# Four PSUM banks for maxima and two for scores, with side work moved to other steps, in a fused FFN-attention-FFN kernel

## The reference

```
x = x + 0.5 * ffn(ln(x))
x = x + attention(ln(x))         # 16 heads of 8, softmax(q k^T / sqrt 8) v, biases, output projection
x = x + 0.5 * ffn(ln(x))
ffn(x): h = silu(x W1 s1) * (x W2 s2)       # 128 -> 512, weights -1, 0, 1 with a scale per column
        h = gelu(h H1 sg1); h = gelu(h H2 sg2)        # 512 -> 512
        return h W3 s3                                # 512 -> 128
```

## Time and profile before

| what | us |
|---|---|
| median of 3 runs (lowest, highest) | 622.78 (621.61, 626.68) |
| the profiled execution | 622.23 |
| its span | 620.3 |
| PE busy, PEld busy | 589.7 (95%), 437.2 (70%) |
| DVE, ACT, POOL busy | 442.0 (71%), 466.3 (75%), 95.4 (15%) |
| mean granted clock | 0.99 |

### The profile page before, as it was taken

How to read it: one execution, slowest core, us unless ns; L and a number is a source line. 1 busy time by engine, 2 the same in 40 slices (tenths; PEclk the granted TensorE clock), 3 DMA queues, 4 the chain that set the end, 5 groups by cost and what they waited for, 6 DMA issues and landing times.

```text
span 620.3 us, 12783 instructions
## 1 busy us (share of the span) xinstructions
PE 589.7 (95%) x4452; PEld 437.2 (70%) x4452; DVE 442.0 (71%) x1048; ACT 466.3 (75%) x794; POOL 95.4 (15%) x258
## 2 busy tenths in 40 slices
PE   2989999999999999999999999999999999999996
PEld 1768878788676666665656565666678878788784
DVE  6885756958646777988979798896575756955742
ACT  4657877968874568787887888787787877968963
POOL 2072020022010312222223222012010020020000
PEclk9999999999999889999999999999999999999999
DMA  8300000000060343452617163400000001000011
GB/s 272 92 1 1 1 2 0 1 0 0 2 241 31 137 137 138 137 189 85 229 59 260 69 205 123 152 2 1 2 1 1 1 1 35 0 22 11 1 34 36
DMA packets 36693, 42.02 MB, mean 68 GB/s; under 512 B 2464, under 2 KB 27296, under 8 KB 36640
## 3 DMA queue, kind: packets, MB, share of 16 engines
q1 hardware_dynamic: 36640, 41.31, 19.8%
HBM read 22.42 MB, written 18.87 MB: 67 GB/s over the span
## 4 chain that ended last, share of the span: by engine, by line
PE 65%; DVE 10%; issue 9%; ACT 9%; POOL 3%; DMA 2%; SPq 1%; POOLq 0%; DVEq 0%; ACTq 0%
PE bank L1083 36%; PE bank L1191 7%; PE bank L1166 6%; PE bank L1178 3%; DVE act_lo L822 3%; DVE silu L831 2%; ACT silu L542 2%; PE bank L1180 2%; DVE neg_max L872 2%; PE bank L1223 2%; ACT act_hi L557 2%; PE bank L1148 1%; PE bank L1152 1%; ACT act_hi L534 1%; PE bank L1209 1%
## 5 line engine op out<-in xcount | busy, mean ns | idle before, releaser
L1083 PE MATMUL bank<-act_hi,WH 128*128 128x512 f32 x576 | 230.2, 400 | 4.3 <-DVE act_lo L822 1.2
L1083 PE MATMUL bank<-act_lo,WH 128*128 128x512 f32 x576 | 225.7, 392 | 0.0
L872 DVE TENSOR_REDUCE neg_max<-bank 128x2 f32<-128x512 f32 x256 | 166.3, 680 | 32.7 <-PE bank L1166 31.6
L842 DVE TENSOR_TENSOR act_lo<-full,act_hi 128x512 fp32r<-128x512 f32 x128 | 91.1, 713 | 111.4 <-ACT act_hi L557 111.2
L672 ACT ACTIVATE probs<-bank 128x512 f32<-128x512 f32 x256 | 139.3, 597 | 36.4 <-PE bank L1180 34.6
L555 ACT ACTIVATE full<-bank,SG 128x512 f32<-128x512 f32 x128 | 88.2, 689 | 68.7 <-PE bank L1083 67.9
L1083 PEld LDWEIGHTS bank<-act_hi,WH 128*128 128x128 f32 x576 | 108.2, 188 | 32.4 <-ACT act_hi L557 4.4
L1083 PEld LDWEIGHTS bank<-act_lo,WH 128*128 128x128 f32 x576 | 108.3, 188 | 22.6 <-issue 0.5
L1178 PE MATMUL bank<-QK 32*128 32x256 f32 x512 | 94.1, 333 | 0.6 <-ACT probs L672 0.4
L557 ACT ACTIVATE act_hi<-bank,SG 128x512 fp32r<-128x512 f32 x128 | 87.3, 682 | 0.0
L1180 PE MATMUL bank<-m_parts,SEL 32*128 32x256 f32 x512 | 80.2, 279 | 0.0
(11 more groups left out here) (95 smaller groups left out, 594.4 us busy)
## 6 DMA issues: line engine op xcount, KB each, us to landing
qk_scratch<-qk SPq DMA_DIRECT2D x64, 256.0 KB, 2.6
QK<-qk_scratch SPq DMA_DIRECT2D x16, 1024.0 KB, 7.1
raw_rest<-w_ffn SPq DMA_DIRECT2D x4, 512.0 KB, 6.6
out<-X SPq DMA_DIRECT2D x4, 512.0 KB, 3.2
X<-x SPq DMA_DIRECT2D x3, 512.0 KB, 7.5
raw<-w_ffn SPq DMA_DIRECT2D x3, 256.0 KB, 4.8
X<-x SPq DMA_DIRECT2D x2, 256.0 KB, 3.0
WA<-w_att SPq DMA_DIRECT2D x1, 256.0 KB, 5.1
```

The source lines that it names most:

```text
L842: D.tensor_tensor(act_lo[1 + layer][:, j, t, :], full[:, t, :], act_hi[1 + layer][:, j, t, :].bitcast(F32), op=ALU.subtract)\
L872: D.tensor_reduce(neg_max[:, bb, qt, n0:n0 + 2], bank[(banks or A_BANKS[bb])[u]][:, :].rearrange("p (h k) -> p h k", h=2), axis=AX.X, op=A ...
L1083: ins = MM(dst, a, b, start=k == 0, stop=k == len(todo) - 1)
```

## The change

- **Banks.** Maxima take banks 0, 1, 5, 3 in turn, scores 2 and 7. All eight banks are in use as before.
- **Steps.** In even batches TensorE's `tokens_of_o` moves from step 13 to 11, with VectorE's `norm_o` and `scale_o` two steps earlier. VectorE's statistics go in two halves at steps 3 and 4 and the rest to 5, 7, 8, 9 instead of 7 to 11; `normalise` comes in three pieces.
- **Entry.** The tokens of the second pair of batches are transposed and projected to q and k inside the third `hidden` of the last body, and to v between the last transposes of y. The first attention batch has no `project_v`; `clear_v(1)` of GpSimd comes behind its first maxima. `qk_full` lies elsewhere in SBUF for that.
- **First body.** ScalarE's last product of layer 1 and the table load for the gelu come before the body, VectorE's last product before the statistics; GpSimd subtracts `WL` in nine pieces instead of five, and the last five wait for `act_lo` of the first hidden layer.

```
-TOKENS = 13
+TOKENS = (11, 13)
...
-A_BANKS = ((0, 1, 5) * 5 + (0,), (5, 1, 0) * 5 + (5,))
-B_BANKS = ((2, 3, 7) * 5 + (2,), (7, 3, 2) * 5 + (7,))
+A_BANKS = ((0, 1, 5, 3) * 4,) * 2
+B_BANKS = ((2, 7) * 8,) * 2
...
-            pool.wait_ge(h_lo, L1_TILES - 1)
-            for k in range(2, len(W_GROUPS)):
-                pool.wait_ge(w_hi, k + 1)
-                pool.tensor_tensor(part_of(WL, k), raw_of(k), part_of(WH, k).bitcast(F32), op=ALU.subtract)\
+            pool.wait_ge(h_lo, L1_TILES)
+            pool.wait_ge(w_hi, len(W_GROUPS))
+            for c in range(C_H1, W_CHUNKS):
+                if c >= C_H2:
+                    pool.wait_ge(g_lo, SLOTS + c - C_H2 + 1)
+                src = raw[:, c:c + 1, :] if c < W_RAW else raw_rest[:, c - W_RAW:c - W_RAW + 1, :]
+                pool.tensor_tensor(WL[:, c:c + 1, :], src, WH[:, c:c + 1, :].bitcast(F32), op=ALU.subtract)\
                     .then_inc(w_lo_rest, 1)
...
-            pool.wait_ge(out_mm, NB)
-            clear_v(1)
...
             max_again(0, 0)
+            pool.wait_ge(out_mm, NB)
+            clear_v(1)
...
-                    side = {0: last_product}
-                    if not first:
-                        side |= {1: lambda: output(before, 0), 2: lambda: output(before + 1, 1)}
+                    if first:
+                        last_product()
+                        load_table(ACT.Gelu)
+                        side = {}
+                    else:
+                        side = {0: last_product, 1: lambda: output(before, 0), 2: lambda: output(before + 1, 1)}
...
-                    hidden(g + 2 * HT, 1, 0)
+                    def entry_q():
+                        full_part(1, 0, 7)
+                        high_part(1, 0)
+
+                    def entry_k():
+                        full_part(1, 1, 6)
+                        high_part(1, 1)
+                    hidden(g + 2 * HT, 1, 0, {0: lambda: x_to_sbuf(1, 6), 2: entry_q, 3: entry_k} if into_att else {})
...
-                    if u == 9 and v_pair is not None:
+                    if u == (9 if prev else 2) and v_pair is not None:
                         set_v(*v_pair)
...
+                    if first:
+                        product_lo(t1, L1_TILES - 1)
                     for step in steps[0:1]:
                         step()
...
-                            entry_max(10, 11, 12, 13, 14, 15)
+                            entry_max(10, 11, 12, 13)
                         residual(nb + 2 * i, 8 * i, 0)
+                        if into_att:
+                            entry_max(14, 15)
                         residual(nb + 2 * i + 1, 8 * i + 4, 1)
...
+                    n = norm_of(q)
+                    even = dict(zip((3, 4, 5, 7, 8, 9), norm_steps(n, 4 * q, 4, halves=True)))
+                    odd = {u: lambda t=t, w=w: normalise(n, 4 * q + t, t, w, last=t == 2)
+                           for u, t, w in ((3, 0, 1), (4, 1, 1), (5, 2, 2))}
...
+                    def entry_q():
+                        entry(1, 2)
+                        pe.wait_ge(x_added, nb + 2 * i + CREDIT)
+                        project_q(1, 7)
+
+                    def entry_k():
+                        entry(3)
+                        project_k(1, 6)
+                    if into_att:
+
+                        pe.wait_ge(x_added, nb + 2 * i - 1 + CREDIT)
+                        transpose_att(1, 4, 6)
                     hidden(g + 2 * HT, 1, 0, g_lo, g + HT + SLOTS, general,
-                           {1: lambda: entry(0), 2: lambda: entry(1, 2), 3: lambda: entry(3)} if into_att else {})
+                           {1: lambda: entry(0), 2: entry_q, 3: entry_k} if into_att else {})
...
                         output(nb + 2 * i, 0, g + 3 * HT, general)
                         if into_att:
+                            entry(10, 11, 12, 13)
+                        output(nb + 2 * i + 1, 1, g + 4 * HT, general)
+                        transpose_y(nb + 2 * i, 0)
+                        if into_att:
+                            entry(14, 15)
                             pe.wait_ge(g_hi, NP * HID_TILES + CREDIT)
-                            transpose_att(1, 4, 4)
-                            entry(10, 11)
-                        output(nb + 2 * i + 1, 1, g + 4 * HT, general)
-                        if into_att:
-                            project_q(1, 5)
-                            entry(12, 13)
-                            project_k(1, 4)
-                            entry(14, 15)
-                        transpose_y(nb + 2 * i, 0)
+                            project_v(1, 4)
                         transpose_y(nb + 2 * i + 1, 1)
...
-                    if u == TOKENS and own and prev:
+                    if u == TOKENS[bb] and own and prev:
...
             def att_body(i, par, ahead=True, more=True, first=False):
-                attend(2 * i, i, par, 0, prev=not first, prev2=not first, v_pair=i + 1 if more else None)
+                attend(2 * i, i, par, 0, prev=not first, prev2=not first,
+                       v_pair=i + 1 if more and not first else None)
```

More of the change, by code:

```diff
@@ L713, in att_body @@
             def att_body(i, par, ahead=True, more=True, first=False):
-                attend(2 * i, 0, prev=not first, prev2=not first, v_pair=(i + 1, 1 - par) if more else None)
+                attend(2 * i, 0, prev=not first, prev2=not first,
+                       v_pair=(i + 1, 1 - par, 4 if first else 6) if more else None)
                 attend(2 * i + 1, 1, prev2=not first, ahead=i + 2 if ahead else None)
@@ L763, in s_stats @@
                         dve.wait_ge(bias_added, biased)
-                    for t in range(width):
+                    for t in range(width // 2 if halves else 0, width):
                         ins = D.bn_stats(stats[:, at + t, :], X[:, bass.ds(tile0 + t, 1), :])
@@ L788, in s_guess, with half_of_stats @@
                                     float(RSQRT_MAGIC), ALU.mult, ALU.add).then_inc(done[4], 1)
-                return [s_stats, s_moments, s_var, s_half, s_guess]
+                def half_of_stats():
+                    for t in range(width // 2):
+                        D.bn_stats(stats[:, at + t, :], X[:, bass.ds(tile0 + t, 1), :])
+                return ([half_of_stats] if halves else []) + [s_stats, s_moments, s_var, s_half, s_guess]
             def first_newton(it, step):
@@ L922, in first_step @@
                     def first_step():
-                        product_lo(t1 + L1_TILES * i, L1_TILES - 1)
+                        if not first:
+                            product_lo(t1 + L1_TILES * i, L1_TILES - 1)
                         for step in steps[1:2]:
@@ L1017, in _, with attend @@
             ffn_phase(0)
-            def attend(b, bb, prev=True, prev2=True, more=True, steps=(), steps_at=7, norm=None, norm_at=3):
+            def attend(b, bb, prev=True, prev2=True, more=True, side={}):
                 for u in range(UNITS):
@@ L1029, in attend @@
                         add_att(b - 2, 2 * b - 4)
[L1030 to L1038 removed]
+                    if u in side:
+                        side[u]()
+                    if u == TOKENS[bb] + 1 and prev:
                         norm_o(b - 1)
[L1040 removed]
+                    if u == TOKENS[bb] + 2 and prev:
                         scale_o(b - 1)
             def att_body(i, par, ahead=True, more=True, first=False):
+                even, odd = {}, {}
                 if ahead:
                     q = i + 2
[L1047 to L1055 removed]
+                    n = norm_of(q)
+                    even = dict(zip((3, 4, 5, 7, 8, 9), norm_steps(n, 4 * q, 4, halves=True)))
+                    odd = {u: lambda t=t, w=w: normalise(n, 4 * q + t, t, w, last=t == 2)
+                           for u, t, w in ((3, 0, 1), (4, 1, 1), (5, 2, 2))}
+                elif not more:
+                    odd = dict(zip(range(2, 7), norm_steps(NORMS1, 0, biased=4)))
+                    odd[10] = lambda: normalise(NORMS1, 0, 0)
+                    odd[11] = lambda: normalise(NORMS1, 4, 4)
+                attend(2 * i, 0, prev=not first, prev2=not first, side=even)
+                attend(2 * i + 1, 1, prev2=not first, more=more, side=odd)
             att_body(0, 0, first=True)
@@ L1111, in hidden @@
                 pe.wait_ge(ready_sem, ready)
+                if general and layer == 1:
+                    pe.wait_ge(w_lo_rest, C_W3 - C_H1)
                 xs = inputs_of(layer, j)
```

51 lines of the change are left out of this document (18 added, 33 removed).

## The result

The changed kernel takes **675.65 us** (median of 4 runs, 667.94 to 680.03), the kernel before beside it 622.19 (4 runs): a ratio of 1.079, with an interval of 1.071 to 1.088. Forecast were 648 us, range 630 to 660. The sign was right, the size was not: +53 us instead of +26, and the range missed. The profiled execution took 677.54 us, with a span of 675.6 and a mean granted clock of 0.946 (before: 620.3 and 0.99).

What follows compares the result with a forecast made beforehand. Attention was taken as bound by the round trip TensorE, ScalarE, score bank. 622.2 + 33 (attention) - 2 (first body) - 4 (entry) = 649, stated as 648 us, range 630 to 660.

Steps and rivals of the forecast that it cites:

- The two score banks: Attention: scores wait for the exp two units back, not three; a group of four units grows by 0.49 to 0.57 us.
- The steps of the group: Attention group: next first scores at 1.51 us, second scores at 2.00, then 0.66 to the weighing, which ends at 3.67.
- the fourth maxima bank: Attention: four banks for maxima can give back at most 1.8 us a pair of batches; taken as 0.
- the first rival: Attention: the maxima were the brake, so four banks make the kernel faster, 606 to 616 us, 612 in the middle; chance 0.10.
- The odd batch's exp behind k: Odd batch, units 12 to 15: ScalarE's work on k stands between two exps and adds 0.5 us, group 4.17.
- Tokens of o at step 11: Even batches: the moved transposes are paid behind a weighing, +0.59 us, while TensorE waits in the gap they leave.
- The clock falls in attention. 0.05: Attention rival: low clock makes a group about 1.7 us longer, in a tenth of 64 groups +11, 660 us; chance 0.05.
- Behind the pairs: After the six pairs: some 13 groups with little side work and two moved transposes, 7.4 + 1.2 = 8.6 us.
- The first body: First FFN body: earlier table load and last product, later and halved subtractions; -2 us, bounds -3.1 and +1.
- VectorE's side work: Attention: other steps and smaller pieces are the same work, covered by TensorE's waits; no cost.
- The entry: Entry into attention: earlier projections give TensorE work and may spare low clock; -4 us.
- The lower bound of -6.5: Entry into attention: the most the new entry was taken to gain, -6.5 us; the other bound was 0.

Runs made afterwards that it cites:

- experiment 1: Kernel before with only the two bank tables changed (four banks for maxima, two for scores): 658.83 us, ratio 1.058.
- experiment 5: Kernel before with only two score banks (2, 7), its three maxima banks kept and bank 3 idle: 663.92 us, ratio 1.064.
- experiment 3: Changed kernel with the transposes of o back at step 13 in even batches, four and two banks kept: 662.22 us, ratio 1.051.
- 2: Changed kernel with the old three and three bank tables; steps, entry and first body as changed: 633.07 us, ratio 1.012.
- 9: Changed kernel with the old bank tables and tokens of o back at step 13, entry as changed: 627.07 us, ratio 1.006.
- experiment 4: Changed kernel with the maxima matmuls of units 2 and 14 issued three times over, also called the filled version: 667.46 us, ratio 1.070.
- experiments 10: Kernel before with the new first body and the new entry, its wait for the residual moved behind the second hidden tile: 620.87 us, ratio 0.997.
- 11: Kernel before with the new entry, its wait moved, and the new first-body order in the first FFN phase only: 618.89 us, ratio 0.9955.
- experiments 8: Kernel before with only the new first body and VectorE's side work at the new steps: 622.84 us, ratio 1.002.

## Why the prediction was wrong in size

- **The two score banks: right.** This is the main cause of the loss, and the mechanism was the forecast one. The steps of the group were forecast at 1.51, 2.00, 2.66 and 3.67 us; they are 1.51, 2.00, 2.65 and 3.65. A pair of batches was forecast at 28.74 + 4.1 = 32.8 and took 32.3 and 32.8. The late weighings stand 3.57 to 3.58 us apart, a little under the 3.67 of the sum. Experiments 1 and 5 show that the lost score bank alone does it. With two score banks the fourth maxima bank gives the 0 that was taken, so the first rival, that maxima were the brake, is out. (Its own sum had a slip: 1.8 x 7 is 12.6 and not 10.)
- **The odd batch's exp behind k: right** in its place: scores that wait for it at 308.98, 2.52 us behind their pair at 306.46.
- **Tokens of o at step 11: right as a cost, wrong as harmless beyond it.** At full clock the move costs 0.55 us a pair (experiment 3) to 0.65 (2 against 9); forecast 0.59. But with two score banks the gap that it leaves is empty, and taking the move back saved 13 us, not 4 (the runs of the two kernels don't overlap).
- **"The clock falls in attention. 0.05": this is the step that failed.** It was the rival with the right mechanism, and the sum took its cost as nothing. Against the prediction's terms the profiled execution lacks 28 us (+55.3 where the unrounded sum has +27.2). Of these 13.5 lie in the five pairs (34.0 for 5 x 4.1): three falls, each a pair of 37.5 us for one of 32.8, are 14. Behind the pairs 6.5 are missing (15.1 for 8.6), of which a low stretch at the end of attention (mean clock 0.66 over 20 us, as much low time as one of those falls) is some 5 by an estimate from what a fall costs in a pair, and the second FFN phase 1.4. The entry with its pair has 8.2 (8.3 for 4.1 - 4).
  The rival was priced at +11 (a tenth of the groups low), where the falls and the low stretch cost some 19, and it was dismissed by a weak comparison: before the old fall TensorE was idle for 1.3 of 2 us, here only 0.75 us of some 4. The page of the Trainium skill that spoke against the change ("TensorE: Matmul & The Clock Gate", psum-queue depth-cycling) tells of short idles between groups of matmuls behind which the clock swings. The trace now agrees with it: a granted clock of 0.50 behind an idle of 0.75 us.
  What the experiments show of the cause is more than the one gap. With the side work back in it, falls come in one pair of five (experiment 3); with useless work there, in two, and short (experiment 4); with the tables alone, in none (experiment 1). But experiment 5 has neither the move nor the long gap, and one short fall; and behind the waits of 0.67 and 0.75 us at 258.85 and 291.32 the changed kernel does not fall. What divides the profiled executions cleanly is the number of score banks. All five with two have low clock near the end of attention, for some 13.6 us (changed kernel), 13.7 (experiment 1), 6.8 (3), 3.4 (4) and 20.5 (5), and four of them have a fall in the five pairs. None with three or four score banks has either. So the record speaks for the waits of the two-bank kernel in general, of which the empty gap is the longest. That this gap alone is the cause is not shown.
- **The first body: right, then lost.** TensorE gained 2.0 us in that stretch and the entry began 2.1 earlier, with no act_lo over 1.80 us where one took 2.90. (The start of the entry also moves by some 3 us from execution to execution: 158.7 to 161.9 us in the kernels with this part, 161.9 to 164.3 in those without.) My sum had the edit in the first FFN phase only; the code says `first`, which the second phase has too, and there the new order costs 1.4 us (experiments 10 and 11).
- **VectorE's side work: 0 was right in the changed kernel.** With two score banks the new steps cost 0.04 us a pair (32.22 in experiment 3, 32.18 in experiment 1), so TensorE's waits do cover them, as forecast. With three banks they cost 0.2 (experiments 8 and 10).
- **The entry: -4 was wrong in sign.** From the entry's start to the second pair's project_v the changed kernel took 8.3 us more. The tables alone have 5.0 there (experiment 1, from 161.9 to 252.0, against 85.1; the sum had some 3.5 of them, in the first of its six pairs), the entry alone 3.7 (experiment 9, 88.8), which together is 0.4 more than the 8.3. Some 3.0 of the entry's 3.7 come before the first scores: 2.68 us of waiting for the residual, and low clock behind it. (The lower bound of -6.5 doesn't follow from the terms given; with all of the low clock gone they add up to -5.4.) The wait stood in the diff, and I priced what it let TensorE do later but not what stood ahead of it: it is a wait in front of a whole hidden layer, for an operation that VectorE reaches only after its share of the half before. Moved by two tiles it costs nothing, and the entry gains 2.2 us on the kernel before (82.9 against 85.1).

What stays open is why, with the same tables, the same order and the same waits, the clock falls in one pair and not in the next, and why the low clock at the start of attention lasted so much longer in experiment 5 than in experiment 1.

## What to carry to other kernels

Count how a ring of banks empties in the grain in which work is issued: here units leave in pairs, so three banks let one half of the next pair go at once and two banks none, for scores (ScalarE) and for maxima (VectorE) alike. A wait that makes TensorE stand empty has two prices, its own length and the clock behind it; where a stall is added to a loop that is full today, give the clock a real chance, and see which side work could stand in the gap. And a new wait is priced by the work behind it on its engine, at every phase that runs the edited line.

## What the runs showed of the hardware

- A gap of 0.75 us, in 15 us in which TensorE was shown busy for 14.25, stands right before a fall from 1.00 to 0.50 of 2.4 GHz, and a wait of 0.27 us right before others (experiments 3 and 5); the same waits stand in pairs without a fall. A fall lasts some 13.5 us: a mean of 0.82 over 37.6 us is (1 - 0.82) x 37.6 / 0.5. In the filled version it is 3.4 us (0.95 over 34.12). It cost 4.8 and 1.3 us.
- The low clock stayed although TensorE was shown busy all the while (14.00 of 14 us at a mean of 0.53, from 325 on).
- The time of one kernel follows its mean clock: the changed kernel's four runs have spans of 666.0, 671.9, 675.6 and 678.1 us at 0.969, 0.956, 0.946 and 0.937.
- Work that nobody needs did not make the kernel slower: 667.5 against 675.7 us in the medians, though the runs overlap at the edge.
- TensorE's busy time rose from 28.13 to 31.82 us for the same matmuls (before, experiment 1). A low idle share is no proof that TensorE is the bound.
